# A second drive buffer for the vector engine, paid for with one of two side banks, in the scan stage of a decoder kernel

## What is computed

```python
delta = softplus(einsum('ble,re->blr', x, wd1) @ wd2.T + wd2_b)
Bm, Cm = einsum('ble,ne->bln', x, wB), einsum('ble,ne->bln', x, wC)
A = -exp(A_log)
def step(h, inp):                       # over the 100 positions
    xt, dt, bt, ct = inp
    h = exp(dt[:, :, None] * A) * h + (dt * xt)[:, :, None] * bt[:, None, :]
    return h, einsum('ben,bn->be', h, ct)
y = swapaxes(ys, 0, 1) + W_D * x
y = y * silu(skip)                      # then the output projection
```

## Time and profile before

| | us |
|---|---|
| median of 3 runs | 2815.17 |
| lowest and highest | 2812.82, 2816.69 |
| the profiled execution | 2815.17 |
| its span in the trace | 2813.2 |
| scan stage in the span | 88.8 to about 534 |
| TensorE busy in the span | 2477.6 |
| VectorE busy in the span | 1384.8 |

### The profile page before, as it was taken

One profiled execution on the slowest core, in us unless ns is written; L12 is line 12 of the kernel. 1 busy time (PEld: TensorE's weight loads), 2 busy tenths in 40 slices (PEclk: granted clock), 3 DMA queues, 4 the chain that ended last, 5 costly groups with the idle time before them and its releaser, 6 DMA issues. The chain is left out here.

```text
span 2813.2 us, 32199 instructions
## 1 busy us (share of the span) xinstructions
PE 2477.6 (88%) x12185; PEld 1240.6 (44%) x12185; DVE 1384.8 (49%) x1950; ACT 908.4 (32%) x1850; POOL 590.7 (21%) x500
## 2 busy tenths in 40 slices
PE   7899999889999999878499899875987679999993
PEld 4344444344555555436245454443664323333331
DVE  5599989422788876621535412385444511111113
ACT  3555565204533335301122110274333112212210
POOL 0366666300000000010201100000000033433333
PEclk9899999999999999989699899997998779999997
DMA  3622222444545444137410100202000242560633
GB/s 103 209 96 87 81 76 87 109 169 151 183 139 169 162 119 159 67 90 240 140 68 0 41 0 3 92 1 90 1 1 1 105 186 90 203 266 23 266 107 113
DMA packets 99256, 301.83 MB, mean 107 GB/s; under 512 B 27468, under 2 KB 57896, under 8 KB 84892
## 3 DMA queue, kind: packets, MB, share of 16 engines
q1 hardware_dynamic: 64012, 171.55, 18.5%
q0 software_dynamic: 35104, 128.36, 12.7%
HBM read 462.51 MB, written 47.21 MB: 181 GB/s over the span
## 5 line engine op out<-in xcount | busy, mean ns | idle before, releaser
L707 POOL TENSOR_TENSOR x_rows<-ms_state,mb_C_everywhere 128x800 f32<-128x800 f32 x128 | 245.1, 1915 | 238.3 <-DVE ms_state L680 151.0
L729 PE MATMUL psum<-mb_context,mb_key_w 128*128 128x361 f32 x768 | 270.9, 489 | 8.2 <-PEq L776 6.4
L957 PE MATMUL psum<-at_Wv,at_context 128*128 128x512 f32 (+1 forms) x576 | 266.2, 601 | 0.0
L680 DVE TENSOR_TENSOR_SCAN ms_state<-ms_decay,psum 128x800 f32<-128x800 f32 x128 | 233.0, 1820 | 27.2 <-ACT ms_decay L627 18.7
L2681 PE MATMUL psum<-tf_W,tf_x_T 128*64 128x512 f32 x1024 | 231.3, 599 | 8.9 <-DMA tf_W<-in_L_W,tt_weight_row 8.9
L2736 ACT ACTIVATE tt_hidden<-psum,tf_b 128x64 f32<-128x64 f32 x512 | 112.0, 330 | 363.8 <-PE psum L2692 363.8
L2703 PE MATMUL psum<-tf_W,tt_hidden 128*64 128x512 f32 x1024 | 226.8, 595 | 0.0
L729 PEld LDWEIGHTS psum<-mb_context,mb_key_w 128*128 128x128 f32 x768 | 139.4, 193 | 142.3 <-issue 45.2
L2626 POOL DMA_INDIRECT tf_W<-in_L_W,tt_weight_row x128 | 127.2, 993 | 229.8 <-PE psum L2681 151.7
L1058 ACT ACTIVATE at_prob<-psum,at_neg_max 100x722 f32<-100x722 f32 x128 | 110.5, 864 | 145.8 <-DVE at_neg_max L1120 145.6
L1120 DVE TENSOR_REDUCE at_neg_max<-psum 100x1 f32<-100x722 f32 x128 | 115.6, 904 | 78.2 <-PE psum L978 77.8
(11 more groups left out here) (456 smaller groups left out, 3764.1 us busy)
## 6 DMA issues: line engine op xcount, KB each, us to landing
at_piece<-in_L_W_f POOLq DMA_DIRECT2D x24, 1024.0 KB
keys_dram<-x_rows SPq DMA_DIRECT2D x128, 180.5 KB, 1.9
at_k_cols<-keys_dram SPq DMA_DIRECT2D x64, 361.0 KB, 3.1
sf_W<-in_L_W SPq DMA_DIRECT2D x16, 1024.0 KB, 7.5
tf_W<-in_L_W SPq DMA_DIRECT2D x8, 2048.0 KB, 23.3
mb_context<-in_ctxT SPq DMA_DIRECT2D x16, 541.5 KB
at_context<-in_ctxT SPq DMA_DIRECT2D x8, 1083.0 KB, 5.1
ternary_dram<-at_piece_made POOLq DMA_DIRECT2D x14, 512.0 KB
```

The source lines that it names most:

```text
L680: nc.vector.tensor_tensor_scan(state[:, n % RH, :], decay[:, g % RA, :, :].rearrange("p b l -> p (b l)"), drive, 0.0, ALU.mult, ALU.add).t ...
L707: nc.gpsimd.tensor_tensor(seen[:, n % RH, :], state[:, n % RH, :], cC[:, n, :], ALU.mult).then_inc(weighed, 1)
L729: last = nc.tensor.matmul(side("key", u, t == KE - 1)[:, 0:SH], lhsT=wk[:, k, e * P:(e + 1) * P], rhs=keys[:, h, k, :], start=(k == 0), st ...
L957: last = nc.tensor.matmul(bank[0:rows_of(t), :], lhsT=ctxT[:, b % 2, k, t * P:t * P + rows_of(t)], rhs=wv[:, k, h * BANK:(h + 1) * BANK], ...
```

## The change

The one `drive` buffer becomes two (`RD` = 2). They and `dx` take 2400 words, so banks 0 to 4. `y` moves to banks 5 and 6, and one bank, 7, is left for side products. On VectorE the multiply for step `n + 1` is issued ahead of the scan of step `n`. Before that multiply stand a wait for multiply `n` (`own.settle()`) and one for scan `n - 1`, which read the buffer that is now rewritten. The multiply of step 0 follows `dx`. TensorE now waits, for each side product, until the product just before it has been taken. `LAG` goes from 4 to 3: ScalarE takes key `n - 3` in step `n`.

```diff
-    RA, RH, RS = 3, 2, 2
+    RA, RD, RH = 3, 2, 2
-        dx, drive = flat[:, 0:T], flat[:, T:2 * T]
-        y, side_banks = [c.banks[4][:, 0:HALF], c.banks[5][:, 0:HALF]], c.banks[6:6 + RS]
+        dx, drive = flat[:, 0:T], flat[:, T:(1 + RD) * T].rearrange("p (r t) -> p r t", r=RD)
+        y, side = [c.banks[5][:, 0:HALF], c.banks[6][:, 0:HALF]], c.banks[7]
-        GATE_AT, LAG = [4, 8], 4
+        GATE_AT, LAG = [4, 8], 3
...
                     own(nc.vector.tensor_tensor(dx, delta[:, j, :], tile_of(xc, i, j), ALU.mult))
+                    dve.wait_ge(scanned, i * per + j * N_ST + RA)
+                    own.add(nc.vector.tensor_tensor(drive[:, 0, :], dx, bC[:, 0, :], ALU.mult))
                     for n in range(N_ST):
                         g = j * N_ST + n
-                        if first and j == 0:
-                            dve.wait_ge(spread[n], 32)
-                        dve.wait_ge(scanned, i * per + g + RA)
-                        own(nc.vector.tensor_tensor(drive, dx, bC[:, n, :], ALU.mult))
+                        own.settle()
+                        if n + 1 < N_ST:
+                            if first and j == 0:
+                                dve.wait_ge(spread[n + 1], 32)
+                            dve.wait_ge(scanned, i * per + g - (RD - 2) + RA)
+                            own.add(nc.vector.tensor_tensor(drive[:, (n + 1) % RD, :], dx, bC[:, n + 1, :], ALU.mult))
                         dve.wait_ge(decayed, i * per + g + 1)
                         dve.wait_ge(weighed, i * per + g + 1)
                         nc.vector.tensor_tensor_scan(state[:, n % RH, :],
                                                      decay[:, g % RA, :, :].rearrange("p b l -> p (b l)"),
-                                                     drive, 0.0, ALU.mult, ALU.add).then_inc(scanned, 1)
+                                                     drive[:, n % RD, :], 0.0, ALU.mult, ALU.add).then_inc(scanned, 1)
...
-            pe.sem_inc(side_taken, RS)
+            pe.sem_inc(side_taken, 1)
```

More of the change, by code:

```diff
@@ L593, in take_key @@
                 act.wait_ge(key_stored[u % 2], t * (8 * N_ST) + 16 * (u // 2) + 16)
-                nc.scalar.copy(made[:, u % 2, :], side("key", u, last)[:, 0:SH]).then_inc(side_taken, 1)
+                nc.scalar.copy(made[:, u % 2, :], side[:, 0:SH]).then_inc(side_taken, 1)
             def take_gate(t, h, last):
@@ L598, in take_gate @@
                 act.wait_ge(side_filled, at_side(t, last, "gate", h) + 1)
-                nc.scalar.copy(gate[:, half(h)], side("gate", h, last)[:, 0:HALF]).then_inc(side_taken, 1)
+                nc.scalar.copy(gate[:, half(h)], side[:, 0:HALF]).then_inc(side_taken, 1)
             def take_delta(t, j, h):
                 act.wait_ge(side_filled, at_side(t, False, "delta", h) + 1)
-                nc.scalar.activation(delta[:, 1 - j, half(h)], side("delta", h)[:, 0:HALF], ACT.Identity,
+                nc.scalar.activation(delta[:, 1 - j, half(h)], side[:, 0:HALF], ACT.Identity,
                                      bias=vec[:, bass.ds(t + 1, 1), DC + 1:DC + 2].rearrange("p a v -> p (a v)")).then_inc(side_taken, 1)
@@ L642, in tile @@
                     if n == OPEN:
-                        act.wait_ge(side_taken, at_side(t, last, "gate", 1) + 1 + RS)
+                        act.wait_ge(side_taken, at_side(t, last, "gate", 1) + 2)
                         nc.scalar.activation(gate, gate, ACT.Silu).then_inc(gated, 1)
@@ L728, in make_key @@
                 for k in range(KC):
-                    last = nc.tensor.matmul(side("key", u, t == KE - 1)[:, 0:SH], lhsT=wk[:, k, e * P:(e + 1) * P], rhs=keys[:, h, k, :],
+                    last = nc.tensor.matmul(side[:, 0:SH], lhsT=wk[:, k, e * P:(e + 1) * P], rhs=keys[:, h, k, :],
                                             start=(k == 0), stop=(k == KC - 1))
@@ L738, in make_gate @@
                     for r in range(2) if h else ():
-                        last = nc.tensor.matmul(side("gate", h, t == KE - 1)[placed(r, h), 0:HALF], lhsT=skipw[:, k, side_of(r)], rhs=c.xT[:, k, half(h)],
+                        last = nc.tensor.matmul(side[placed(r, h), 0:HALF], lhsT=skipw[:, k, side_of(r)], rhs=c.xT[:, k, half(h)],
                                                 start=(k == 0), stop=(k == KD - 1))
                     if not h:
-                        last = nc.tensor.matmul(side("gate", h, t == KE - 1)[:, 0:HALF], lhsT=skipw[:, k, :], rhs=c.xT[:, k, half(h)],
+                        last = nc.tensor.matmul(side[:, 0:HALF], lhsT=skipw[:, k, :], rhs=c.xT[:, k, half(h)],
                                                 start=(k == 0), stop=(k == KD - 1))
@@ L747, in make_delta @@
                 pe.wait_ge(side_taken, at_side(t, False, "delta", h) + 1)
-                nc.tensor.matmul(side("delta", h)[:, 0:HALF], lhsT=wd2[:, (t + 1) * P:(t + 2) * P], rhs=proj[:, half(h)],
+                nc.tensor.matmul(side[:, 0:HALF], lhsT=wd2[:, (t + 1) * P:(t + 2) * P], rhs=proj[:, half(h)],
                                  start=True, stop=True).then_inc(side_filled, 1)
```

12 lines of the change are left out of this document (6 added, 6 removed).

## The result

The changed kernel took 2861.27 us (median of 4 runs, 2858.72 to 2865.32) against 2815.26 us for the kernel before on the same chips (2812.82 to 2816.69). The ratio is 1.0166, with a 95% interval of 1.0148 to 1.0183: the change costs 46 us. The forecast was 2870 us, in a range of 2836 to 2898. The profiled execution took 2864.09 us, with a span of 2862.3.

A forecast was written before the change was run, and what follows sets the result against it. TensorE was taken to set the scan stage's pace, busy 53.4 of 54.0 us a tile. Losses of 23.4 + 12.1 + 7.4 + 10.6 + 1.0 = 54.5 us on 2815.2 gave 2870 us, range 2836 to 2898.

The forecast's parts named there:

- VectorE's gain: Multiply and scan hand-overs on VectorE: a step saves between nothing and some 0.25 us, costed at nothing because TensorE hides it.
- Gates and deltas: The key after each waits for ScalarE to empty the bank: 0.72 or 0.85 us each, 23.4 us together.
- Ordinary keys: Keys with an `add` before the next key: hand-over free, 0.21 us left, as long as ScalarE stands ready.
- rival C: Every key's copy is exposed, up to 0.56 us a key, 72 us more, up to 2942 us; chance 0.06.
- The long chains on ScalarE: Last curve delays key 11 by 1.73 us (12.1 us in all), Silu delays key 13 by 0.93 us (7.4 us).
- Rival A: Only waits after gates and deltas are paid; ScalarE's late chains and `finish` are absorbed: 2840 us; chance 0.15.
- The end of a tile: TensorE waits for `finish` before `add` 0: 2.2 us against 0.69, 1.5 us more at seven ends, 10.6 us.
- SP and the first tile: Row requests for B and C costed at nothing; one more multiply ahead of the very first scan costs 1.0 us.
- round trips: TensorE's waits for ScalarE to empty the one side bank after gates and deltas: 23.4 us together.
- B: TensorE's granted clock falls to 0.50 in the middle of the stage; time just under 2898 us; chance 0.12.
- D: Faster: ScalarE's copies cost TensorE nothing, VectorE's gain is left, about 11 us, 2804 us; chance 0.04.
- E: No change in the kernel's time: losses are much smaller and VectorE's gain pays for them; chance 0.03.

## Why the prediction was right, and where it wasn't

**What bounds the stage: right.** TensorE sets the pace, and nearly all that was taken from it is lost: 6.12 us a steady tile. VectorE's gain bought nothing there: 60.13 us with it, 59.97 without.

**Gates and deltas: right.** Forecast 3.14 us a tile and 23.4 in all. The stops measure 0.85, 0.79 and 0.72 us; with the slower keys behind them 3.5 us a tile, 25.5 us when tried alone.

**Ordinary keys: right.** In the steady tiles not one of them waits; rival C is out. (One does between tiles 0 and 1, for 2.27 us, behind the late rows.)

**The long chains on ScalarE: right in size.** Forecast 1.73 and 0.93 us, measured 1.74 and 1.06: the `add` ahead of the `add` of `xc` advances TensorE by 0.72 us, not the 0.84 that I took, and the kernel before shows this too. Rival A, in which they are absorbed, is out: in the changed kernel both stops are there in full. The wait for `finish` gives a part back, 0.95 us of 2.80 when tried alone.

**The end of a tile: wrong.** The step that failed is "the end of a tile", where I put 10.6 us. Measured is 0.56 us of waiting for `finish` a tile (2.8 us in five) against 0.75 (4.5 in six), so about 1 us less in all, not 10.6 more. The last scan came when I said, 396.71 - 391.68 = 5.03 us after the end of key 11 (forecast 5.02). But from there to the end of `finish` it is 11.46 us, not 13.1. Of the 1.6 us, 1.35 are `dx`, which I carried over at 2.32 us from the earlier trace rows; that number was no price of the instruction but its meeting with a POOL product, and in the new schedule, with `LAG` = 3, they don't meet. The rest, 0.3 us, is that the hand-overs gave back more than I allowed.

**The first tile: wrong, the other way.** In "SP and the first tile" I wrote that a multiply now wants its row a scan earlier, and costed it at nothing, on the ground that TensorE had no gap there while VectorE waited. That step failed as well. The waits for rows went from 12.7 to 24.3 us, TensorE then stood for POOL (8.3 us in 4 waits, 4.7 in 2 before) and its clock fell at two places instead of one; up to the first `finish` it is 10.5 us, of which the old order with one bank has 1.0.

So the two errors, about 11 us too much at `finish` and about 10 too little in the first tile, nearly cancel. That is luck: the 54.5 us look better than their parts. The stage's 49.9 us are: round trips and chains 6 x 6.31, `finish` 6 x -0.19, the first tile 10.5, the last 2.7.

**Rivals.** B is out for the steady tiles, whose granted clock is 1.00: stops of 1.66 and 0.99 us 7.4 us apart left it alone. It fell only in and behind the first tile, at two places. And the fall that I had taken from the earlier trace rows to need two stops came behind the first of them, the one of 2.52 us: the `add` between the two already took 1.35 us instead of 0.90. D's mechanism, the copies hidden, is refuted by the 45 waits, and E by the 46 us.

## What to carry to other kernels

Before giving a buffer to an engine, ask whether that engine sets the pace of the stage, and who pays: here the giver was the bound, with 0.7 us of slack in 54. The second side bank earned its place where two products follow each other with nothing between (3.5 us a tile), and where ScalarE has a long operation to do first (2.8 us); behind an ordinary key, with an `add` between, one bank did as well. And a duration read in one schedule is not the price of the instruction in another, if another engine's instruction overlaps it: `dx` took 2.32 us in one and 0.97 in the other.

## What the hardware showed that I had not expected

- `dx` (two SBUF inputs) started beside a POOL product takes 2.32 us, alone 0.97; it ends 0.86 us behind the POOL product. The other way round, a POOL product started beside `dx` takes 2.19 instead of 1.91 us, and in the kernel before (149.46) 2.54.
- Three key matmuls straight behind a delta or the first gate take 1.99 us, behind an `add`, the second gate or a stop 2.09, at the same granted clock of 1.00. Why isn't known.
- TensorE's granted clock fell from 1.00 to 0.50 behind single waits of 2.52 us (before) and 2.67 us (after, 129.51), about 0.4 and 1.1 us after TensorE had started again. It stayed at 1.00 with waits of 1.66 and 0.99 us in every steady tile.
- A scan with no wait on the multiply ahead of it starts 0.09 us before that one's end; with the wait a step is 0.135 us longer.
